# Linear attention with decay and a quantised linear layer on one core: VectorE normalises the columns of x in two operations instead of GpSimd in eight, and the steps between and behind the two phases are reordered

## The reference

```python
xn = layernorm(x)                                  # over the 512 features
q, k, v = elu(xn @ Wq) + 1, elu(xn @ Wk) + 1, xn @ Wv
a = sigmoid(xn @ Wa + ba + 2)                      # one decay per token and head
S = a * S + k v^T;  z = a * z + k                  # along the tokens
x = x + ((q S) / (q z + 1e-6)) @ Wo
x = x + (layernorm(x) @ CB^T) * (SCB / 127) + bias
```

## Time and profile before

| what | value |
|---|---|
| median of 3 runs | 1969.92 us (1967.62 to 1970.51) |
| the profiled execution's own time | 1968.92 us |
| its span, first to last instruction | 1967.1 us |
| granted TensorE clock, mean | 0.997 |

### The profile page before, as it was taken

One profiled execution on the slowest core, in us unless ns is written; L12 is line 12 of the kernel. 1 busy time (PEld: TensorE's weight loads), 2 busy tenths in 40 slices (PEclk: granted clock), 3 DMA queues, 4 the chain that ended last, 5 costly groups with the idle time before them and its releaser, 6 DMA issues.

```text
span 1967.1 us, 69099 instructions
## 1 busy us (share of the span) xinstructions
PE 1939.7 (99%) x26926; PEld 1691.0 (86%) x26926; DVE 1643.5 (84%) x2918; ACT 686.3 (35%) x1288; POOL 389.9 (20%) x368
## 2 busy tenths in 40 slices
PE   7999999999999999999999999999989999999998
PEld 6888888888888888888888889888878888888887
DVE  8788888888888888888888888888777777777776
ACT  5333343334443343334334433443422222222221
POOL 3222222232222223322222223222010000000000
PEclk9999999999999999999999999999999999999999
DMA  6344443444344544443434444435466666666664
GB/s 216 89 94 97 100 114 96 109 106 109 93 97 99 115 95 110 105 109 95 97 98 111 99 110 105 104 101 129 105 159 163 161 161 161 160 161 161 160 160 113
DMA packets 596067, 237.40 MB, mean 121 GB/s; under 512 B 432064, under 2 KB 546240, under 8 KB 596032
## 3 DMA queue, kind: packets, MB, share of 16 engines
q1 hardware_dynamic: 560896, 204.94, 43.9%
q10 hardware_dynamic: 35136, 32.00, 5.6%
HBM read 168.59 MB, written 51.97 MB: 112 GB/s over the span
## 4 chain that ended last, share of the span: by engine, by line
PE 95%; DMA 1%; SPq 1%; issue 1%; DVE 1%; ACT 0%; POOLq 0%; POOL 0%; DVEq 0%; ACTq 0%
PE G L1320 54%; PE DS L1278 17%; PE NUM L1278 8%; PE NUM L1389 4%; PE SC L1442 3%; PE DS L1421 3%; PE NUM L1403 3%; PE SC L1268 2%; PE DS L1462 1%; DMA qs<-in_Wq 0%; DMA attn_cols<-attn 0%; SPq L429 0%; DMA norm_rows<-moments 0%; DMA out_rows<-xt 0%; DVE D L1106 0%
## 5 line engine op out<-in xcount | busy, mean ns | idle before, releaser
L1320 PE MATMUL G<-w_hi,xT_hi 128*128 128x512 f32 x1024 | 406.9, 397 | 1.3 <-DVE w_lo L912 1.3
L1320 PE MATMUL G<-w_lo,xT_hi 128*128 128x512 f32 x1024 | 399.8, 390 | 0.0
L1320 PE MATMUL G<-w_hi,xT_lo 128*128 128x512 f32 x1024 | 399.0, 390 | 0.0
L734 ACT ACTIVATE relu_t<-G 128x512 f32<-128x512 f32 x256 | 153.1, 598 | 452.5 <-PE G L1320 449.5
L1320 PE MATMUL G<-xT_hi,w_hi 128*128 128x256 f32 x1024 | 290.3, 283 | 0.2 <-DVE w_lo L912 0.2
L1320 PE MATMUL G<-xT_lo,w_hi 128*128 128x256 f32 x1024 | 289.9, 283 | 0.0
L1320 PE MATMUL G<-xT_hi,w_lo 128*128 128x256 f32 x1024 | 289.8, 283 | 0.0
L1320 PEld LDWEIGHTS G<-w_hi,xT_hi 128*128 128x128 f32 x1024 | 192.4, 188 | 42.9 <-DVE xT_lo L905 1.4
L1320 PEld LDWEIGHTS G<-w_hi,xT_lo 128*128 128x128 f32 x1024 | 192.3, 188 | 41.3
L1320 PEld LDWEIGHTS G<-w_lo,xT_hi 128*128 128x128 f32 x1024 | 192.6, 188 | 35.7
L702 ACT ACTIVATE w_hi<-at_rows 128x512 fp32r<-128x512 f32 x128 | 73.8, 624 | 386.5 <-PE DS L1278 380.7
(11 more groups left out here) (137 smaller groups left out, 3602.0 us busy)
## 6 DMA issues: line engine op xcount, KB each, us to landing
abc<-decay_rows SPq DMA_DIRECT2D x256, 128.0 KB, 3.3
pbc<-product_rows SPq DMA_DIRECT2D x256, 128.0 KB, 3.1
attn_cols<-attn SPq DMA_DIRECT2D x512, 64.0 KB, 2.2
at_rows<-attn_cols ACTq DMA_DIRECT2D x244, 128.0 KB, 2.8
xt<-in_x SPq DMA_DIRECT2D x64, 256.0 KB, 3.2
x_in<-in_x SPq DMA_DIRECT2D x64, 256.0 KB, 3.0
out_rows<-xt SPq DMA_DIRECT2D x64, 256.0 KB, 3.0
xT_in<-in_xT SPq DMA_DIRECT2D x31, 512.0 KB, 4.4
```

Source lines behind the costliest of these rows:

```text
L734: act.activation(relu_t[buffer][:, :], bank[:, :], ACT.Relu)
L1320: made = nc.tensor.matmul(to, lhs, rhs, start=(n == 0), stop=(n == len(passes) - 1))
```

## The change

VectorE gets two functions, `centred_columns` and `normal_columns`, each one operation over all 1024 elements of a partition (the same row of `bias_b` is read for each of the four tiles), in the b = 0 step: one ahead of `elu_q(2, 1)`, one behind `decay_matrix(0)`. GpSimd's eight operations go. `norm_rows` is stored as [4, 128] instead of [128, 4], so that the two rows that are read together lie side by side in `bias_b`; the store then writes every number to a place of its own. In the passage `residual_normal(1, 0)` and `rows_lo(3, 0)` stand ahead of `normalised(1)`, and ScalarE rounds the turned rows of chunk 0 ahead of its `rows_hi`. In the tail the last chunk's moments come ahead of `with_bias`, a y ahead of `turned_lo(NC)`, and each of the last y waits for the store two chunks back.

```diff
-    norm_rows = nc.dram_tensor("norm_rows", [C, 4], fp32).ap()
+    norm_rows = nc.dram_tensor("norm_rows", [4, C], fp32).ap()
...
-        norm_b = bias_b[:, :].rearrange("p (c s a) -> p a s c", s=2, a=2)
+        norm_b = bias_b[:, :].rearrange("p (s a c) -> p a s c", s=2, a=2)
+        x_tiles = xT_in[:, :, :].rearrange("p k (s c) -> p k s c", s=2)
...
-                    sp.dma_start(norm_rows, moments[:, :, :].rearrange("p s a -> p (s a)")).then_inc(norm_stored, 16)
+                    sp.dma_start(norm_rows.rearrange("m c -> c m"), moments[:, :, :].rearrange("p s a -> p (s a)"),
+                                 allow_slow_non_contiguous=True).then_inc(norm_stored, 16)
...
-                    for kt in range(KT):
-                        made = pool.tensor_tensor(x4[:, kt, :, :], x4[:, kt, :, :], norm_b[:, 0, :, :], ALU.subtract)
-                    made.then_inc(xT_centred, 1)
-                    pool.wait_ge(xT_centred, pairs[0])
-                    for kt in range(KT):
-                        made = pool.tensor_tensor(x4[:, kt, :, :], x4[:, kt, :, :], norm_b[:, 1, :, :], ALU.mult)
-                    made.then_inc(xT_normal, 1)
+                    inverse_deviation(counts(pool, pair, 1, (1,))[1])
...
+                if isinstance(i, int) and i == 2:
+                    turned_hi(1, 0)
                 if exists(i + 1):
                     rows_hi(r64[1], one[-1], 1 - b)
...
                 dve.wait_ge(stats2_ready, count)
-                if biased is not None:
+                last = isinstance(count, int) and count == NC
+                if biased is not None and not last:
                     with_bias(biased)
...
+                if last:
+                    with_bias(biased)
...
+                def over_tiles(a):
+                    return norm_b[:, a:a + 1, :, :].broadcast_to([128, KT, 2, C])
+                def centred_columns():
+                    dve.wait_ge(xT_loaded, x16[0])
+                    dve.wait_ge(norm_loaded, x16[0])
+                    nc.vector.tensor_tensor(x_tiles, x_tiles, over_tiles(0), ALU.subtract).then_inc(xT_centred, 1)
+                def normal_columns():
+                    dve.wait_ge(xT_centred, pairs[0])
+                    nc.vector.tensor_tensor(x_tiles, x_tiles, over_tiles(1), ALU.mult).then_inc(xT_normal, 1)
...
+                    if exists(i + 2):
+                        centred_columns()
                     elu_q(2, 1)
                     decay_matrix(0)
+                    if exists(i + 2):
+                        normal_columns()
                     elu_q(3, 0)
...
+                    residual_normal(1, 0)
+                    rows_lo(3, 0)
                     normalised(1)
...
-                if isinstance(i, int) and i == NC:
-                    turned_lo(NC, 1 - b)
                 if exists(i - 3):
...
-                        wait(dve, y_stored, y16[-4])
+                        wait(dve, y_stored, y16[-5 if isinstance(i, int) and i > LAST else -4])
                     nc.vector.tensor_tensor(y[1 - b], F[1 - b], x1b[1 - b], ALU.add).then_inc(y_ready, 1)
                 if isinstance(i, int) and i == NC:
+                    turned_lo(NC, 1 - b)
```

More of the change, by code:

```diff
@@ L516, in spread_norm @@
                     wait(sp, xT_normal, pairs[-1])
-                    sp.dma_start(bias_b[:, :], norm_rows.rearrange("(q c) m -> q (c m)", q=1).broadcast_to([128, 4 * C]))\
+                    sp.dma_start(bias_b[:, :], norm_rows.rearrange("(q m) c -> q (m c)", q=1).broadcast_to([128, 4 * C]))\
                         .then_inc(norm_loaded, 16)
@@ L850, in turned_hi @@
                     act.activation(by_stretch(fT_hi[of]), both_of(TF), ACT.Copy).then_inc(fT_hi_ready, 1)
+                if isinstance(i, int) and i == 2:
+                    turned_hi(1, 0)
                 if exists(i + 1):
                     rows_hi(r64[1], one[-1], 1 - b)
-                if isinstance(i, int) and i == 2:
-                    turned_hi(1, 0)
-                elif exists(i - 2):
+                if exists(i - 3) and exists(i - 2):
                     act.wait_ge(fT_loaded, r64[-3])
@@ L1202, in step2 @@
                 x16 = counts(dve, i, 16, (0,))
-                y16 = counts(dve, i, 16, (-4,))
+                y16 = counts(dve, i, 16, (-5, -4) if isinstance(i, int) else (-4,))
                 r64 = counts(dve, i, 64, (-4,))
@@ L1209, in turned_lo @@
                                             ALU.subtract).then_inc(fT_lo_ready, 1)
-                if exists(i - 1):
+                opening = isinstance(i, int) and i == 1
+                if exists(i - 1) and not opening:
                     residual_normal(one[-1], 1 - b)
@@ L1220, in step2 @@
                                         x1n[1 - b].rearrange("p (b f x) -> p x b f", f=SQ, x=4)).then_inc(x1t_ready, 1)
-                if exists(i + 1):
+                if exists(i + 1) and not opening:
                     rows_lo(one[1], 1 - b)
```

## The result

The changed kernel takes 2209.48 us (median of four runs, 2201.36 to 2212.39), against 1970.06 us for the kernel before beside it. The ratio is 1.1208, with a 95% interval of 1.1194 to 1.1221: 12% slower, where I had forecast 1964.6 us and a small gain. The profiled execution has a span of 2210.6 us.

A forecast was written before the change was run, and what follows sets the result against it. TensorE, busy 1939.7 of 1967.1 us, was taken as the bound, with gains only in its stops and half-clock stretches. Terms 0 + 0.8 + 2.7 + 1.8 = 5.3 us gave a median of 1964.6, range 1961.0 to 1967.3.

The forecast's parts named there:

- The store of norm_rows: Store of 512 separate numbers: covered in the steady loop, 0.3 us more at the first pair, bounds 0 and 2.2.
- the steady pairs' operations: Phase one's steady pairs: two added VectorE operations, at most 2.8 us, are covered; value 0, bounds 0 and 1.8 a pair.
- the passage: Passage: TensorE no longer waits for k but stops anew some 3.4 us; gain 2.7 us, bounds 1.1 and 4.3.
- the tail: Tail: last rows come 0.6 us earlier and last y waits for its product; gain 1.8 us, bounds 1.2 and 2.0.
- the 0.8 of the first pair: First pair: TensorE's stop shrinks from 3.0 to 2.2 us; gain 0.8, bounds a loss of 1.1 and a gain of 2.6.
- just at the edge: Steady pairs, if the store came 6.6 us later under the skill's rule: cover barely enough; first pair 6 us worse; not expected.
- VectorE becomes what TensorE waits for in each pair: Rival in the steady pairs: k late in each of 31 pairs, up to 1.8 us a pair, 2020 us; chance 0.05.

The follow-up runs named there:

- the probes: Six variants of the kernel before, each with one more store per pair that nobody waits for, differing in where the numbers go: 1971.58 to 2164.07 us.
- the probe: Kernel before plus one more store per pair of 512 single 4-byte numbers side by side, with nobody waiting before the end: 2164.07 us.
- the operations alone: Kernel before with the two column operations on VectorE, GpSimd's eight gone, old norm_rows layout and old order of passage and tail: 1969.61 us.
- the order alone: Kernel before with only the reordered passage and tail, columns on GpSimd and old norm_rows layout: 1964.61 us.
- the last kernel: Reordered passage and tail on the kernel before, plus chunk 1's residual work moved ahead of attn's transpose and chunk 0's bias addition moved later: 1963.96 us.
- all but the store: Changed kernel with norm_rows stored as [128, 4] again, in 128 runs of four numbers: 1965.20 us.
- its store alone: Kernel before with only the layout of norm_rows changed, so the store writes 512 numbers apart: 2185.07 us.

## Why the prediction was wrong

The step that failed is "The store of norm_rows". It had 0.3 us in all, at the first pair alone, and costs 244 (2209.48 less 1965.20), 7.9 a pair: the sum priced only the wait for the store, and what the store costs is a hold-up of TensorE that needs no wait. Of the other steps the steady pairs' operations and the passage came out near their numbers, the tail at 1.5 of 1.8, and the 0.8 of the first pair wasn't found. In the words of the prediction:

- *"Nearest are the stores of attn, 64 KB in short runs, which land 2.2 us after their issue"*. The row is right and stands for something else. Those runs have 32 numbers each, by the code of `store_rows`; the probes show that 16 bytes in place of 4 takes 6.3 us a pair down to 0.1. I had compared sizes in all and counts, and not how long a single run is and how close the next one lies.
- *"as data of four times the count is still only 2 KB"*. Neither the 2 KB nor the count makes the price: the same 2 KB in pieces of 16 bytes, and the same count 64 bytes apart, cost 0.1 us a pair.
- *"the bounds are 0 and a whole further landing, 2.2"*. What waits for the store started 9.1 us behind its issue at the first pair (30.84 to 39.95) and 11.3 in the pair shown; the old one had landed after 4.29. A bound taken from a row of another kind was no bound.
- *"in the steady loop the load that waits for the store is held 1.75 us longer by another wait"*. That cover was read rightly from its row. But cover was the wrong question: it protects who waits for the store, and the probe shows 6.3 us of loss with nobody waiting.

The Trainium skill, "DMA: Bandwidth & Descriptors", section "Rules for kernel authors", had warned of one descriptor per element for such a store. I weighed the rule and turned it down with the earlier trace rows. The changed kernel's page agrees: 11904 packets more on SP's queue (572800 against 560896), 384 for each of the 31 stores, which is 512 in place of 128. Following the rule would have been right. But the number of descriptors isn't what makes the price here: 512 single numbers 64 bytes apart cost 0.1 us a pair. And the price I worked out from it, 6.6 us on the store's landing, would still have put the steady pairs "just at the edge", and not at 7.9 us each.

The other steps, by the experiments:

- **Steady pairs: nothing.** Right for the operations. They cost 1.22 and 1.20 us in the changed kernel (L1083, L1088, 31 each), in the range of 1.2 to 1.4; the scan D is at 1203 ns over all 128; and the operations alone leave TensorE busy for 1189.99 of the 1190 us.
- **First pair: 0.8.** Not found, and too small to be told in single executions: in the order alone and in the last kernel, which change nothing there, TensorE's stop is 2.16 and 2.15 us, against 3.01 in the kernel before. In the changed kernel the late store swallows it, and with the old store the numbers lie 16 bytes apart for VectorE, which reads them at another price (timeline of VectorE, the operations alone):

```profile
41.21 1.97 DVE L1079 TENSOR_TENSOR xT_in<-xT_in,bias_b 128x1024 f32<-128x1024 f32 x1
...
44.84 1.95 DVE L1084 TENSOR_TENSOR xT_in<-xT_in,bias_b 128x1024 f32<-128x1024 f32 x1
```

  That is 3.9 us instead of 2.4, and TensorE's stop there is 2.88, against 3.01. So the packed rows do make the operations cheaper, by 1.5 us a pair; but VectorE has that much to spare in the steady pairs.
- **Passage: 2.7.** Held. No wait for k; a new one ahead of NUM of 3.0 us in the changed kernel and in the order alone, 3.8 in all but the store, where I had said 3.4. In the order alone the way from the turn of chunk 0 to NUM is 9.13 us (1439.51 to 1448.64), in all but the store 9.98, and before 13.83 (1440.81 to 1454.64). Counted on to the next product with the second matrix (1462.80 before, 1458.53 and 1461.60), so with what the clock costs in it, 3.0 and 2.1 us are gained, on both sides of the 2.7.
- **Tail: 1.8.** 1.5 measured. In all but the store the last y starts 0.43 us behind the last matmul (1961.28 and 1960.85), before 1.64: 1.2 gained there. Ahead of it only 0.2 of the 0.6 came: from the y three before the last one to the last normalised rows (tile k) it is 5.79 us (1948.48 to 1954.27), before 6.01 (1949.67 to 1955.68). The moments come 0.6 earlier, but `with_bias` now stands between them and k, and VectorE still waits 0.44 us for GpSimd behind it. From the same y to the last one it is 12.80 us, before 14.28. That it would wait for its product alone was wrong: it still waits 2.03 us for a store, only this one is done in time.

Together, with the old store: 4.0 us measured (1969.18 less 1965.20), where 5.3 less the 0.8 of the first pair was forecast. Of the rivals "VectorE becomes what TensorE waits for in each pair" had the right sign and place and the wrong cause: between 160 and 1350 us no row of TensorE's waits in the changed kernel names VectorE. Range and chances were too narrow because the one operation of which I had no row was priced by the one that looked most like it.

What stays open: how the store holds up TensorE. The trace shows that TensorE stops with "issue" while VectorE works on until it needs TensorE, and that the DMA share is 0.00 meanwhile. That writes of single numbers into one small piece of DRAM are worked off one by one, and that something TensorE needs from DRAM stands behind them, is a guess that would fit. No run shows it. Open too are the 0.9 us a pair by which the changed kernel is dearer than its store alone (7.9 and 7.0), though the rest of its change wins time.

## What to carry to other kernels

When an edit changes the layout of something in DRAM, work out for the writing side how long one contiguous run is and how close the next lies, and not the bytes and the count alone; single 4-byte numbers side by side are to be avoided even if nobody waits for them (here 4.4 and 6.3 us for each store of 128 and 512). Where such a layout is wanted for its reader, price the reader's gain first: here it was 1.5 us of an engine that wasn't the bound. And if no row of the trace shows an access pattern, the honest upper bound is not the nearest row of another pattern; a probe that does the operation with no one waiting costs one run.

## What the runs showed of the hardware that I had not expected

- A store of 2 KB as 512 single numbers side by side takes 9 to 11 us from its issue to its reader's start, and during it TensorE stops with nothing to wait for that the profile names, for up to 7.0 us in the probe with the same pattern (`NUM L1408 <- issue: 56.9, 17, 7.0`).
- 128 such numbers, 512 bytes in all, still cost 4.4 us a pair; 512 at 16 bytes' distance 0.6, at 64 bytes' 0.1.
- Like stops don't bring like clocks. In the passage TensorE was granted half speed behind 2.45, 2.99 and 3.85 us. Behind the first pair's stop the clock stayed full in the order alone (2.16 us; 1.00 in the window from 50 to 53) and was at half in the last kernel (2.15 us; 0.50 in the same window). The two differ in nothing there, and half speed over those 3 us is worth 1.5, by my estimate.
- VectorE takes 1.97 us instead of 1.22 for the same 1024 elements a partition when the operand that is spread over the tiles has its numbers 16 bytes apart.
